# Macaron layer on one core: TensorE takes a unit's three down products between its gate and its up products

## The reference

```python
def ffn(x):                                  # x: layer-normed tokens [T, 128]
    scores = sigmoid(x @ router_w.T)         # 16 experts in 4 groups
    # best 2 groups by the sum of their two best (scores + bias), best 4 experts in them
    combine = one_hot(topk_idx, 16) * (scores / sum * 2.5)
    h = einsum('td,edf->etf', x, gate_w); u = einsum('td,edf->etf', x, up_w)
    y = einsum('etf,efd->etd', silu(h) * u, down_w)
    routed = einsum('etd,te->td', y, combine)
    shared = silu(x @ sh_gate_w) * (x @ sh_up_w) @ sh_down_w     # 256 wide
    return routed + shared

x = x + 0.5 * ffn(layernorm(x))
x = x + attention(layernorm(x))   # 32 heads of 4, no softmax, group norm over the sequence
x = x + 0.5 * ffn(layernorm(x))
```

## Time and profile before

| | us |
|---|---|
| median of 3 runs | 751.8 (751.61 to 751.99) |
| the profiled execution's own time | 755.5 |
| its span | 753.8 |
| PE busy | 680.1 |
| DVE busy | 592.5 |
| POOL busy | 432.1 |
| ACT busy | 397.6 |
| mean granted clock of TensorE | 0.965 of 2.4 GHz |

### The profile page before, as it was taken

The page is one execution under the profiler, slowest core; times in us unless marked ns, Lnnn a source line. Parts: engine busy times, 40 slices in busy tenths (PEclk is TensorE's granted clock), DMA queues, the critical chain, the costliest instruction groups (busy, mean ns, idle before and its releaser), DMA issues.

```text
span 753.8 us, 12004 instructions
## 1 busy us (share of the span) xinstructions
PE 680.1 (90%) x3116; PEld 555.4 (74%) x3116; DVE 592.5 (79%) x1571; ACT 397.6 (53%) x784; POOL 432.1 (57%) x373
## 2 busy tenths in 40 slices
PE   3498989989898988989979989799897999989897
PEld 2287778878787877778867878678686878878675
DVE  3898696878887697886878878878788797878674
ACT  3464645555573543755436554366553655555453
POOL 4555655666673553855547455475553766666564
PEclk9799999999998998999989999899998999999999
DMA  6640606041230601405006051050410606041240
GB/s 189 191 168 2 224 1 225 1 180 46 98 129 0 225 2 31 195 0 224 0 5 221 0 194 45 3 223 14 174 65 0 225 15 225 15 168 72 66 174 15
DMA packets 30789, 76.37 MB, mean 101 GB/s; under 512 B 3968, under 2 KB 12688, under 8 KB 30736
## 3 DMA queue, kind: packets, MB, share of 16 engines
q1 hardware_dynamic: 30736, 75.81, 28.0%
HBM read 73.18 MB, written 2.62 MB: 101 GB/s over the span
## 4 chain that ended last, share of the span: by engine, by line
PE 33%; DVE 21%; issue 20%; POOL 18%; DMA 4%; ACT 2%; POOLq 1%; SPq 0%; DVEq 0%; ACTq 0%
POOL A_lo L323 16%; DVE T L952 6%; DVE A L974 5%; PE gateP L410 4%; PE gateP L412 3%; PE gateP L411 3%; PE yP L410 3%; PE yP L411 3%; PE yP L412 3%; PE upP L412 3%; PE upP L411 3%; PE upP L410 3%; DMA CB<-combT 2%; DVE wsum L841 2%; DMA ebias<-in_L_ffn_bias_dram 1%
## 5 line engine op out<-in xcount | busy, mean ns | idle before, releaser
L323 POOL TENSOR_TENSOR A_lo<-A,A_hi 128x512 fp32r<-128x512 f32 x288 | 371.5, 1295 | 252.7 <-ACT A_hi L673 252.6
L656 ACT ACTIVATE gateP<-gateP 128x512 f32<-128x512 f32 x256 | 149.0, 582 | 232.1 <-PE gateP L412 231.6
L952 DVE TENSOR_TENSOR T<-gateP,CB 128x512 f32<-128x512 f32 x256 | 175.3, 685 | 103.9 <-ACT gateP L656 81.1
L673 ACT CAST A_hi<-A 128x512 fp32r<-128x512 f32 x288 | 176.6, 613 | 42.6 <-DVE A L974 42.6
L974 DVE TENSOR_TENSOR A<-upP,T 128x512 f32<-128x512 f32 x256 | 177.0, 691 | 9.1
L410 PE MATMUL gateP<-XT_hi,W_hi 128*128 128x512 f32 x288 | 124.6, 433 | 3.5 <-DVE T L952 3.1
L410 PE MATMUL yP<-A_hi,W_hi 128*128 128x512 f32 x288 | 115.0, 399 | 1.5 <-ACT YT L589 0.9
L410 PE MATMUL upP<-XT_hi,W_hi 128*128 128x512 f32 x288 | 115.5, 401 | 0.3
L412 PE MATMUL gateP<-XT_lo,W_hi 128*128 128x512 f32 x288 | 115.4, 401 | 0.0
L411 PE MATMUL gateP<-XT_hi,W_lo 128*128 128x512 f32 x288 | 115.3, 400 | 0.0
L412 PE MATMUL upP<-XT_lo,W_hi 128*128 128x512 f32 x288 | 114.6, 398 | 0.0
(11 more groups left out here) (169 smaller groups left out, 671.6 us busy)
## 6 DMA issues: line engine op xcount, KB each, us to landing
CB<-combT SPq DMA_DIRECT2D x128, 512.0 KB, 7.1
out_dram<-X SPq DMA_DIRECT2D x8, 256.0 KB, 2.0
X<-in_L_attn_x_dram SPq DMA_DIRECT2D x3, 512.0 KB, 6.1
W_in<-in_L_ffn_gate_w_dram SPq DMA_DIRECT2D x4, 256.0 KB, 5.3
W_in<-in_L_ffn_up_w_dram SPq DMA_DIRECT2D x4, 256.0 KB, 5.3
W_in<-in_L_ffn_down_w_dram SPq DMA_DIRECT2D x4, 256.0 KB, 5.4
X<-in_L_attn_x_dram SPq DMA_DIRECT2D x2, 256.0 KB, 3.7
combT<-CT SPq DMA_DIRECT2D x16, 32.0 KB, 1.8
```

The costliest lines, as they stand in the source:

```text
L323: pool.tensor_tensor(A_lo[:, slot, :], A[:, slot, :], A_hi[:, slot, :].bitcast(F32), ALU.subtract).then_inc(low_done, 1)
L656: act.activation(dst, gateP[u % 2][:, :], ACT.Silu).then_inc(silu_done, 1)
L673: act.copy(A_hi[:, v % SLOTS, :], A[:, v % SLOTS, :]).then_inc(high_done, 1)
L952: dve.tensor_tensor(T[:, u % TS, :], gateP[u % 2][:, :], CB[:, e, :], ALU.mult).then_inc(gate_weighted, 1)
```

## The change

In every unit PE now issues gate(u), down(u-4), up(u), where it issued gate(u), up(u), down(u-4). The waits go with their products; no instruction is added or removed, and the other engines' programs stay as they are. Units 0 to 3 of the first step have no down products, and the four closing rounds of the last pair have nothing else.

```diff
-                        left = gate_left(t0 + (u - 2) // UNITS, (u - 2) % UNITS)
-                        for i, (dst, done, left) in enumerate(((gateP[u % 2], gate_done, left),
-                                                               (upP[u % 2], up_done, (mul_done, n + u - 1)))):
-                            if not (first and u < 2):
-
-                                pe.wait_ge(*left)
-                            product(dst[:, :], W_hi[:, w, i, :], W_lo[:, w, i, :], XT_hi[:, s, :],
-                                    XT_lo[:, s, :], True, True).then_inc(done, 1)
+                        if not (first and u < 2):
+
+                            pe.wait_ge(*gate_left(t0 + (u - 2) // UNITS, (u - 2) % UNITS))
+                        product(gateP[u % 2][:, :], W_hi[:, w, 0, :], W_lo[:, w, 0, :], XT_hi[:, s, :],
+                                XT_lo[:, s, :], True, True).then_inc(gate_done, 1)
                     if not (first and u < LAG):
                         down(n, u - LAG, t0 + (u - LAG) // UNITS)
+                    if u < PAIR:
+                        if not (first and u < 2):
+
+                            pe.wait_ge(mul_done, n + u - 1)
+                        product(upP[u % 2][:, :], W_hi[:, w, 1, :], W_lo[:, w, 1, :], XT_hi[:, s, :],
+                                XT_lo[:, s, :], True, True).then_inc(up_done, 1)
```

## The result

| | before | after |
|---|---|---|
| median of 6 runs, us | 751.9 (751.0 to 765.3) | 770.9 (768.2 to 772.4) |
| the profiled execution's own time, us | 755.5 | 769.2 |
| its span, us | 753.8 | 767.5 |
| its mean granted clock | 0.965 | 0.966 |

The changed kernel is slower: ratio 1.0248, 95% interval 1.0223 to 1.0274, some 19 us. I had forecast 760.1 in a range of 754.5 to 767.

A forecast was written before the change was run, and what follows sets the result against it. PE, busy 90% of the span, was taken to bound the kernel, waiting on DVE for comb and zb. Terms 1.3 + 3.4 + 1.6 + 0.4 = 6.7, with the clock 8.3, on the median 751.8 gave 760.1 us, range 754.5 to 767.

The forecast's parts named there:

- What is removed: Whole kernel: only order changes; a possible gain from up products' waits for A, at most 3.2 us, was counted as nothing.
- Term 1: Unit 8 of each step: the later up product delays A(8) by 0.08 us, 16 times, 1.3 us.
- Term 2: Unit 4: down(0), issued earlier, waits for the YT copy with up(4) behind it; 3.4 us in five steps, 1.6 in four.
- Term 3: Behind the zb wait, at half clock: A(15) and comb 1.28 us later, PE still in time; 0.1 in four steps, 0.4 us.
- Term 4: PE's clock: shifted waits add one short half-clock spell, 1.6 us, between -1.6 and +3.2.

The follow-up runs named there:

- e8: Changed kernel with the old order kept in units 4 and 8 and in the unit behind the wait for zb; one execution, 752.0 us.
- e7: Changed kernel with the YT copy on ACT moved from the head of unit 4 to behind the silu of unit 3; 762.9 us, ratio 1.013.
- e2: Changed kernel with the old order kept in unit 4 of every step; 764.9 us, ratio 1.014.
- e1: Kernel before with the new order in unit 4 of every step only; 761.9 us, ratio 1.013.
- e10: e1 with the YT copy on ACT moved to behind the silu of unit 3; 756.1 us, ratio 1.005.
- e3: Kernel before with the new order only in the unit behind zb, in the second step of the four attention pairs; 764.7 us, ratio 1.0145.
- e5: e3 plus a wait on POOL, so that behind zb A_lo(15) starts only when comb is done; 757.7 us, ratio 1.006.
- e9: Changed kernel with the old order kept only in the unit behind the wait for zb; 763.6 us, ratio 1.015.
- e4: Changed kernel with the old order kept in unit 4 and in the unit behind the wait for zb; 755.5 us, ratio 1.003.
- e11: Changed kernel with the YT copy moved behind unit 3's silu and POOL's A_lo(15) held until comb is done in every step; 743.6 us, ratio 0.989.
- e12: Kernel before with the YT copy moved behind unit 3's silu and POOL's A_lo(15) held until comb is done in every step; 741.9 us, ratio 0.987.

## Why the prediction was wrong

The direction and the four places were right; the size was not, 8.3 us against 19.

- **What is removed: nothing.** Right. No run shows a gain of the new order.
- **Term 1, A later by 0.08 us per step, 1.3 us.** Right in mechanism and near in size: 0.10 to 0.12 per step, paid once per step, at A(8), as e8 shows. Only in the second steps of the attention pairs there is another 0.17 to 0.20 us between gates 9 and 14, 0.7 in all, which goes with unit 8 as well (e8); I have not followed it further. It needed no more than two rows: when T ends, and when the product that moved would.
- **Term 2, the YT copy, 5.0 us.** Right in mechanism and near in size: between gates 0 and 5 the trace after is 4.4 us longer in sum, 5.1 without step 0. Without that step e7 takes 4.3 of it away, and e2 3.6. My assignment of steps was worse than the total: step 3 was to cost nothing and costs 0.5, step 1 was to cost 0.68 and is 0.43 shorter, because the `CB` transfer lands at other times in other executions (in step 1 T(2) waited 2.7 us for it before and 1.0 after). Such a cost belongs to an expectation over steps, not to numbered steps. e1's rest, 7.0 above before, does not show that the term was too small: e1 has a wait of its own, as e10 shows, and the rest is good to 2 or 3 us.
- **Term 3, behind zb, 0.4 us. This is the step that failed.** I had A(15) 1.28 us later, correctly (1.2 to 1.3 in e3), and `comb` 1.28 later with it, and PE "in time, by 0.1". Two things were wrong in it. First, the room of step 5 was taken for all four steps; in steps 7, 9 and 11 it was 0.4 to 0.7 us smaller than the delay, 1.8 us in all, which the trace of before would have shown. Second, the chain was moved as if its operations kept their durations. But moved by 1.28 us it ran into POOL's A_lo(15), which had come behind it before, and in three of the four steps `comb` became 0.96 to 0.98 us longer, 2.9 us in all. e5 shows this as POOL's doing. e3 measured 5.5 us in its trace, above even my upper end of 5.1, since that end had no collision in it; some 0.2 us in each step stay unexplained. In the changed kernel's trace the four steps cost 4.0 us, with 3.4 us less half clock behind `zb` in steps 5 and 7; at equal half clock, by e8's prices of 1.3 and 0.8 us for these, that is 6.1, an estimate. The warning was in the trace: an operation of the same kind, `wsum`, took 1.14 us in eleven places and 0.17 in the five others, the second steps of the attention pairs among them. I looked at the row's place and not at its spread.
- **Term 4, the clock, 1.6 us.** Too small: 10 us more at half clock than before, 4.7 us. I had read three runs within 0.4 us as a pattern that repeats. It does not: thirteen runs of before range over 9 us with the clock. The Trainium skill's sentence that the monitor's window is free-running (TensorE: Matmul & The Clock Gate, Part 1: The HAM clock gate), which I had set aside, is what these runs agree with. That kernels with more or longer waits of PE (after, e3, e9) lay at 56 to 60 us and some with fewer (e4, e11) at 36 to 43 is seen but was not tested by itself; e7, at 47 with all the waits for `comb`, and e12, at 51 with short waits, speak against a simple rule. The cause of the 10 us stays open.

In sum, as estimates from the runs: 1.6 (term 1 and its attention part), 4.4 to 5 (term 2), 6 (term 3), 4.7 (term 4), some 17 us. That is also the distance of the means, 770.6 against 753.5 for the thirteen runs of before; the runs of before beside the result had a mean of 752.0, which makes it 19.

## What to carry to other kernels

When a term is read in one place and charged in several, read its room in each of them. When a change moves a chain of small operations in time, check what the other engines run at the new time, above all GpSimd beside VectorE: an operation's duration is not its own if its row shows two values (minimum and median far apart). A product that is issued earlier pays only if its inputs are ready earlier; a wait that moves ahead of independent work takes that work with it, so before moving one, list who else stands in the releaser's queue. And on a kernel with many short stalls, compare runs with their granted clock beside them, or three agreeing runs will be taken for precision.

## What the runs showed of the hardware

Two small VectorE operations, `wsum` and `comb`, of 0.17 and 0.27 us, did not end before GpSimd's A_lo had ended when they started while it ran: `wsum` 1.14 us (ended at 195.26, A_lo at 195.24), `comb` 1.23 and 1.25 us (0.13 to 0.14 behind A_lo's end). Other VectorE operations keep their time beside it: T and A, the large products that read PSUM, 0.63 to 0.69 us with it and without, and the FIND_INDEX8 of the routing (L826), as short as `wsum`, 0.17 us in all its 64 places. So it depends on the operation. The Trainium skill (SBUF — State Buffer, SBUF: two separate sides) says this: an exclusive lock on a port pair shared by the two engines, held for a whole instruction, taken by whichever starts first, and not touched by VectorE operations without a fast mode or a second SBUF input. The rows agree as far as they go; they show GpSimd holding it, not VectorE. To hold GpSimd back by one wait showed no cost here, as its result is wanted four units later, and gave 11 us.
